# The keys of the last long attention block, made in closed tiles of 128 keys: 15 and 32 of them inside two earlier attention cores, 17 in pauses of other blocks

## The reference, cut to what matters

```python
h = layer_norm(x, g_norm)
q = h @ Wq                                 # 16 heads of 64
k, v = split(context @ Wkv)                # 2048 keys and values per batch, plus one null key and value
q, k = l2norm(q) * q_scale, l2norm(k) * k_scale
sim = einsum('bhid,bhjd->bhij', q, k) * 8.0
out = einsum('bhij,bhjd->bhid', softmax(sim), v) @ Wout
x = x + layer_norm(out, g_out)
```

## Time and profile before

| what | value |
|---|---|
| median of 3 runs | 1338.66 us (1333.35 to 1340.05) |
| the profiled execution, its own time | 1339.16 us |
| its span, first to last instruction | 1337.4 us |
| mean granted TensorE clock | 0.893 of full speed |
| PE busy | 1158.4 us, 87% of the span |
| DVE, ACT, POOL busy | 548.9, 467.1 and 434.3 us |

### The profile page before, as it was taken

The page is one execution under the profiler, slowest core; times in us unless marked ns, Lnnn a source line. Parts: engine busy times, 40 slices in busy tenths (PEclk is TensorE's granted clock), DMA queues, the critical chain, the costliest instruction groups (busy, mean ns, idle before and its releaser), DMA issues.

```text
span 1337.4 us, 15482 instructions
## 1 busy us (share of the span) xinstructions
PE 1158.4 (87%) x6398; PEld 689.3 (52%) x6398; DVE 548.9 (41%) x949; ACT 467.1 (35%) x638; POOL 434.3 (32%) x217
## 2 busy tenths in 40 slices
PE   7999967799686998987885697799999999999558
PEld 4645533265265654543472585555565555555334
DVE  2212357413344632336213512444554454454445
ACT  3344531233132554441241101544434444344111
POOL 0355500000000155520000000288687678677000
PEclk9899968899587899986896687899999999999769
DMA  8333300002000143330007003031311312210100
GB/s 350 140 144 140 142 0 1 0 1 94 33 0 1 40 158 134 126 142 0 0 1 330 0 1 126 1 126 64 126 64 64 126 64 81 109 63 1 69 0 9
DMA packets 23830, 102.74 MB, mean 77 GB/s; under 512 B 2768, under 2 KB 2768, under 8 KB 19920
## 3 DMA queue, kind: packets, MB, share of 16 engines
q1 hardware_dynamic: 23760, 101.76, 19.8%
HBM read 67.93 MB, written 33.82 MB: 76 GB/s over the span
## 4 chain that ended last, share of the span: by engine, by line
PE 77%; DVE 9%; issue 8%; ACT 4%; POOL 2%; DMA 0%; POOLq 0%; DVEq 0%; ACTq 0%
PE PSUM L1958 18%; PE PSUM L1897 10%; PE PSUM L1445 9%; PE PSUM L1534 3%; PE PSUM L1471 3%; PE PSUM L1454 2%; PE PSUM L1625 2%; PE PSUM L1636 2%; PE PSUM L1489 2%; PE PSUM L2000 1%; DVE ARENA L930 1%; PE PSUM L1822 1%; PE PSUM L1590 1%; PE PSUM L1832 1%; PE PSUM L1495 1%
## 5 line engine op out<-in xcount | busy, mean ns | idle before, releaser
L447 POOL TENSOR_TENSOR CK<-CK,ARENA 128x2048 f32<-128x2048 f32 x63 | 285.1, 4526 | 126.3 <-ACT ARENA L691 122.2
L1958 PE MATMUL PSUM<-ARENA,CT 128*128 128x512 f32 x512 | 239.7, 609 | 0.0
L1290 DVE TENSOR_TENSOR ARENA<-PSUM,RK 128x512 f32<-128x512 f32 x256 | 159.1, 684 | 186.6 <-PE PSUM L1897 186.5
L691 ACT ACTIVATE ARENA<-ARENA,WB 128x1024 f32<-128x1024 f32 x128 | 147.0, 1148 | 203.3 <-DVE ARENA L1290 200.6
L385 POOL TENSOR_TENSOR RSTD<-VE,MHALF 128x4 f32<-128x4 f32 x17 | 17.1, 1008 | 478.9 <-DVE VE L766 412.4
L1897 PEld LDWEIGHTS PSUM<-ARENA 64*128 64x128 f32 x2048 | 120.9, 190 | 50.7 <-issue 47.0
L1958 PEld LDWEIGHTS PSUM<-ARENA,CT 128*128 128x128 f32 x512 | 91.8, 190 | 99.3 <-issue 91.2
L1897 PE MATMUL PSUM<-ARENA 64*128 64x128 f32 x2048 | 133.2, 281 | 2.5 <-ACT WB L686 2.2
L1445 PE MATMUL PSUM<-CT,WK 128*128 128x512 f32 x256 | 126.8, 622 | 2.4 <-ACT W L471 1.8
L1445 PEld LDWEIGHTS PSUM<-CT,WK 128*128 128x128 f32 x256 | 43.3, 192 | 64.0 <-issue 29.5
L1429 PE MATMUL PSUM<-WA,HN 128*128 128x128 f32 x52 | 12.9, 396 | 63.4 <-DVE HN L769 49.5
(11 more groups left out here) (396 smaller groups left out, 1805.5 us busy)
## 6 DMA issues: line engine op xcount, KB each, us to landing
ARENA<-kept_keys SPq DMA_DIRECT2D x16, 2048.0 KB, 7.8
kept_keys<-KEYS SPq DMA_DIRECT2D x64, 256.0 KB, 2.0
kept_keys<-W SPq DMA_DIRECT2D x64, 256.0 KB, 2.0
CT<-in_ctxT SPq DMA_DIRECT2D x4, 1024.0 KB, 9.9
CK<-in_l0f_experts SPq DMA_DIRECT2D x1, 4096.0 KB, 22.9
CK<-in_ctxk SPq DMA_DIRECT2D x1, 4096.0 KB, 12.4
ARENA<-in_l2f_experts SPq DMA_DIRECT2D x2, 2048.0 KB, 8.4
CT<-in_ctxk SPq DMA_DIRECT2D x1, 4096.0 KB, 26.5
```

Source lines behind the costliest of these rows:

```text
L447: nc.gpsimd.tensor_tensor(LS[b % 2], LS[b % 2], PR[:, t % 2, :], ALU.add)\
L691: act(p, p, ACT.Exp, bias=SHIFT).then_inc(sem("l3x_probs"), AC.sends("l3x_probs"))
L1290: ve.tensor_tensor(PR[:, k, q * 512:(q + 1) * 512].rearrange("p (j n) -> p j n", j=4), bank(q).rearrange("p (j n) -> p j n", j=4), each(rk ...
L1958: last = mm(bank(4 + q), CTK[:, t, :], PR[:, t % 2, q * 512:(q + 1) * 512], start=k == 0, stop=k == KEY_TILES - 1)
```

## The change

The unit of work becomes a tile: 128 context rows through all eight chunks, in two halves of four matmuls of 128x128 (`key_rows`), each half filling one PSUM bank. The 64 tiles are each closed by themselves: squares of both halves, their sums in eight 32-column matmuls of 128 columns (`sum_squares`, one tile late), one transpose (`turn_norms`), and one ScalarE copy for each of the last two. `places` says where the tiles are made: 15 in the core of l0x (one for each group), 32 in the core of l1a (two for each group), 17 in pauses: three in l0a, l1x (three), ahead of l1a (two), l1f (two), l2x (one), l2a (two) and l2f (four). In l0a, ahead of l1a, in l2a and l2f they stand between the block's output and `turn_pe`, and there ScalarE squares all but the last tile itself.

There are two buffers of a whole tile for the kept keys, in place of four of a unit, and one buffer of squares for each half, in place of six in turn. Stores to HBM become 64 of 512 KB, and a load back reads four runs of 4 KB for each partition instead of one of 16 KB. The load of the last two experts of l2f into `W8` (1 MB of expert weights) and that of the contexts into `CT` move behind the last keys, as those buffers are still in use. The root and the reciprocal of the norms (`RK`) move into l2f, the latter in quarters between copies. At the end of l3x the last sums take 32 rows for each strip in one bank (L2046, L2053 of the new file), are inverted in two pieces of 256 columns, and are spread afterwards by eight small matmuls of one row (`spread_last`).

```diff
-            def key_rows(units):
-                for n in units:
-                    if n >= 2:
-                        nc.tensor.wait_ge(sem("keys_kept"), n - 1)
-                    mm(bank(5 + 2 * (n % 2)), WK[:, (n % 8) * P:(n % 8 + 1) * P], CT[:, (n // 8) * 512:(n // 8 + 1) * 512],
-                       start=True, stop=True).then_inc(sem("key_rows"), PE.sends("key_rows"))
...
+            def key_rows(s, h, bank_k):
+                if 2 * s - 1 + h > 0:
+                    nc.tensor.wait_ge(sem("keys_kept"), 2 * s - 1 + h)
+                for j in range(4):
+                    c = 4 * h + j
+                    last = mm(PSUM[:, bank_k, j * P:(j + 1) * P], WK[:, c * P:(c + 1) * P], CT[:, s * P:(s + 1) * P],
+                              start=True, stop=True)
+                last.then_inc(sem("key_rows"), PE.sends("key_rows"))
+
+            def sum_squares(s, bank_k):
+                nc.tensor.wait_ge(sem("key_squares"), 2 * s + 2)
+                if s:
+                    nc.tensor.wait_ge(sem("key_norm_rows"), s)
+                for r in range(2):
+                    for j in range(4):
+                        last = mm(PSUM[32 * j:32 * j + 32, bank_k, 0:P], w("l3x_pick")[:, 32 * r:32 * r + 32],
+                                  key_squares_of(s, r)[:, j * P:(j + 1) * P], start=r == 0, stop=r == 1, skip_group_check=True)
+                last.then_inc(sem("key_squares_added"), PE.sends("key_squares_added"))
+
+            def make_tile(s, banks, first=False):
+                a, b, n = banks
+                key_rows(s, 0, a)
+                if not first:
+                    sum_squares(s - 1, n)
+                key_rows(s, 1, b)
+                if not first:
+                    turn_norms(s - 1, n)
+
+            def make_before_turn(place, banks, first=False):
+                tiles = places[place]
+                for s in tiles[:-1]:
+                    make_tile(s, banks, first and s == tiles[0])
+                key_rows(tiles[-1], 0, banks[0])
+                key_rows(tiles[-1], 1, banks[1])
+                sum_squares(tiles[-1] - 1, banks[2])
...
             tail_pe(w("l0x_WoT"))
+            make_before_turn("l0a", (4, 5, 6), True)
...
             turn_pe()
+            turn_norms(places["l0a"][-2], 6)
...
+        L0X_TILES = 15
+        places, at = {}, 0
+        for place, n in (("l0x", L0X_TILES), ("l0a", 3), ("l1x", 3), ("l1a_norm", 2), ("l1a", 32),
+                         ("l1f", 2), ("l2x", 1), ("l2a", 2), ("l2f", 4)):
+            places[place] = range(at, at + n)
+            at += n
...
+            def keep_tile(s, banks, first, square=()):
+
+                a, b, n = banks
+                keep_key_rows(s, 0, a)
+                if 0 in square:
+                    square_keys(s, 0)
+                if not first:
+                    keep_key_sums(s - 1, n)
+                keep_key_rows(s, 1, b)
+                if 1 in square:
+                    square_keys(s, 1)
+                if not first:
+                    keep_key_norms(s - 1, n)
...
+            def key_squares(tiles, halves=(0, 1)):
+                for s in tiles:
+                    for h in halves:
+                        nc.gpsimd.wait_ge(sem("keys_kept"), 2 * s + 1 + h)
+                        if s:
+                            nc.gpsimd.wait_ge(sem("key_squares_added"), s)
+                        kept = KEEP_T[s % 2][:, h * 512:(h + 1) * 512]
+                        nc.gpsimd.tensor_tensor(key_squares_of(s, h), kept, kept, ALU.mult).then_inc(sem("key_squares"), 1)
...
                 for k in range(2):
-                    half = slice(k * 512, (k + 1) * 512)
-                    ve.reciprocal(L9INV[:, half], bank(k)).then_inc(sem("dve_step"), DV.sends("dve_step"))
...
+                    half = slice(k * 256, (k + 1) * 256)
+                    ve.reciprocal(L9INV[:, half], PSUM[:, 0, half]).then_inc(sem("l3x_inverted"), DV.sends("l3x_inverted"))
```

More of the change, by code:

```diff
@@ L308, in build, with key_squares_of, key_steps @@
         PICK2 = ARENA[0:16, 2048 + PAIRS * 3 * P:2048 + PAIRS * 3 * P + 16 * DH]
-        def key_plan(n0):
-            plan, n, added = [], n0, n0 // 4
-            for g in range(16):
[L315 to L322, removed]
+        def key_squares_of(s, h):
+            return KSQ_FIRST if h == 0 else HT[:, :] if s < L0X_TILES else WA[:, 272:784]
+        L0X_TILES = 15
[4 more added lines that the diff above has]
+            at += n
+        assert at == TILES
+        def key_steps(place):
+            left = list(places[place])
+            steps = []
+            for g in range(16):
+                if len(left) > 16 - g:
+                    steps.append((left[0], left[1]))
+                    left = left[2:]
+                else:
+                    steps.append((left[0], None) if left else (None, None))
+                    left = left[1:]
+            return steps
         SUMS_AT, VALUES_AT, OUT_AT = 0, 2, 7
@@ L346, in _, with keep_keys @@
             load(CK[:, :, :].rearrange("p a b -> p (a b)"), d["l0f_experts"], "dma_experts")
[L348 to L354, removed]
+            def keep_keys(first, last):
+                for t in range(places[first][0], places[last][-1] + 1):
+                    nc.sync.wait_ge(sem("keys_kept"), 2 * t + 2)
+                    sync.dma_start(d["keys"][t], KEEP_T[t % 2]).then_inc(sem("dma_keys%d" % (t % 2)), 16)
+            keep_keys("l0x", "l0a")
             nc.sync.wait_ge(sem("x_ready"), SP.due("x_ready", n=3))
             load(CK[:, :, :], d["ctxk"], "dma_ck")
-            keep_keys(64)
+            keep_keys("l1x", "l1a")
             nc.sync.wait_ge(sem("x_ready"), SP.due("x_ready", n=2))
-            load(W8[:, :], d["l2f_experts"][:, 14 * NW:16 * NW], "dma_moe8_early")
             load(ARENA[:, 14336:14336 + 4 * NW], d["l2f_experts"][:, 0:4 * NW], "dma_moe8_early")
+            keep_keys("l1f", "l2x")
             nc.sync.wait_ge(sem("x_ready"), SP.due("x_ready", n=2))
@@ L417, in _ @@
             norm_pool()
+            key_squares(places["l1x"], (0,))
             norm_pool()
[L421 removed]
+            key_squares(places["l1a_norm"][-1:])
+            key_squares(places["l1a"])
+            norm_pool()
+            key_squares(places["l1f"], (0,))
+            norm_pool()
+            key_squares(places["l2x"])
+            norm_pool()
+            key_squares(places["l2a"][-1:])
             norm_pool()
             norm_pool()
[L430 to L434 removed]
+            key_squares(places["l2f"][-1:])
             nc.gpsimd.wait_ge(sem("l3x_null_square"), PO.due("l3x_null_square"))
@@ L489, in core_act, with keep_before_turn @@
+            def keep_before_turn(place, banks, first=False):
+                tiles = places[place]
+                for s in tiles[:-1]:
+                    keep_tile(s, banks, first and s == tiles[0], square=(0, 1))
+                keep_key_rows(tiles[-1], 0, banks[0])
+                keep_key_rows(tiles[-1], 1, banks[1])
+                keep_key_sums(tiles[-1] - 1, banks[2])
             def core_act(groups, scale, plan=None):
                 for g in range(groups):
-                    first, second, halves, turned = plan[g] if plan else ([], [], [], [])
+                    one, two = plan[g] if plan else (None, None)
+                    last = plan and g == 15 and one is None
@@ L509, in probs @@
                         accum_out=LSUM[:, b:b + 1]).then_inc(sem("long_probs"), AC.sends("long_probs"))
+                for s in places["l1x" if masked else "l2x"]:
+                    keep_tile(s, (4, 5, 6), False, square=(1,) if masked else ())
                 probs(0)
@@ L616, in _ @@
                     .then_inc(sem("l1f_hidden_kept"), AC.sends("l1f_hidden_kept"))
+            for s in places["l1f"]:
+                keep_tile(s, (3, 4, 0), False, square=(1,))
             context_keys_act(KT, w("l2x_bk"), c0=CHUNKS // 2)
@@ L1499, in long_pe @@
                 scores(0)
+                mine = places["l1x" if masked else "l2x"]
+                for s in mine:
+                    make_tile(s, (4, 5, 6))
                 for b in range(B):
```

250 lines of the change are left out of this document (157 added, 93 removed).

## The result

The changed kernel takes 1291.28 us (median of 4, 1287.32 to 1294.27) against 1337.5 of before beside it (4 runs); the ratio is 0.9656, 95% interval 0.9618 to 0.9693. The prediction was 1295. The profiled execution of after is its fastest (1287.32, span 1285.5), that of before was above its median, so the two traces lie 51.9 us apart where the medians lie 46.2 apart.

The account below looks back on a forecast made before the run. The prediction took TensorE, with 77% of the chain's busy time, to bound the kernel. From a median of 1338.66 us, -42 + 9 - 7 - 4.4 = -44.4 gave 1295 us, range 1277 to 1323.

Parts of the forecast that it names:

- Core l0x: In l0x's core, fifteen tiles (41.0 us) replace 78.1 us of key work and 5 us of idle TensorE return: -42 us.
- Core l1a: In l1a's core, 32 tiles take 87.4 us for 78.1, stalls shrink, waits for squares come: +9 us, 0 to +21.
- Pauses: Seventeen tiles in the seven pauses: overruns cost +10 us, the clock kept up behind them gives -17, together -7.
- End of l3x: At l3x's end: sums in four strips -1.7 us, halved reciprocals -3.3, spreading adds some .6: -4.4, -5 to -3.
- At nothing: Doubled stores, loads back in 4 KB runs, later `W8` and `CT` loads, and `RK`'s root and reciprocal were put at no cost.
- Low clock in the pauses: All seventeen pause tiles run at 1.2 GHz: +49 us, 1351; at half strength 1323. Chance .03 in full, .06 at half.
- Small matmuls dearer per column: Half a tile costs over 1.42 us, so the kernel ends slower; 1373 us at twice L1636's price. Chance .02.
- A cold core: Cores l0x and l1a granted 1.2 GHz: a group takes 5 us longer in l0x, 8 in l1a. Chance .03.
- Another engine in l0x: Each group of l0x's core has a floor of 6.2 us, so the change saves 20 us less: 1315. Chance .06.
- Costly tiles: In the cores, a tile of 3.1 us, with .99 for keys and sums, adds 19 us: 1314. Chance .10.

Follow-up runs that it names:

- e5: The changed kernel run again as it is, beside three that go on from it: 1288.43 us, 0.9601 of the kernel before.
- e10: The changed kernel with the squares of l1f's two tiles made by ScalarE alone, none by GpSimd there: one run, 1290.1 us.
- e1: The kernel before with matmuls that nobody reads in its seven pauses and no key work moved: 1323.23 us, ratio 0.9843.
- e2: The changed kernel with all 64 tiles in the two cores, 32 in l0x and 32 in l1a, none in pauses: 1355.24 us, 1.0101 of before.
- e4: The changed kernel with ScalarE, not GpSimd, squaring the second half of each group's first tile in l1a's core: 1289.16 us, 0.9607 of before.
- e6: The changed kernel with one of l1a's 32 tiles made ahead of the turn of l1x's tokens: 1288.62 us, 0.9603 of before.

## Why the prediction was right, term by term

*Core l0x: -42 forecast, -43.9 measured.* The step that TensorE bounds it, and that nothing else sets a group of 4.95 us, held (4.85). A tile was 2.46 us with .15 behind it in place of 2.73: the lower bound of the working, with the exit from strips that it had left out.

*Core l1a: +9, measured +6.0.* The stall for the single buffer of squares was there at .39 a group, where .3 was put. The tile there was dearer than in l0x, by the .2 that follows strips and short scores, yet TensorE's busy time rose by 6.4, not by 9.3. In e5's profile, at a clock of .96, the core is 10.6 us longer than before, so the term lies between two profiles of one kernel.

*Pauses: -7.* The rest of the 51.9 between the profiles is -51.9 + 43.9 - 6.0 + 1.6 - 1.3 = -13.7. Overruns were forecast for l0a, l1a and l2f at 2.9, 3.5 and 3.0 and were 1.9, 1.6 and 2.8. The one of l1x, put at .2, was 3.6: there a sum waits 2.4 us for GpSimd's squares. l1f, l2x and l2a are over by 1.6, .7 and .8, in l1f partly for a reason that the working lacked, VectorE beside GpSimd (e10). That is 13 where 10 were put down, and leaves some 27 for the clock in place of 17, while e1 gives 18 without keys. By e5's profile the rest is -12.6 instead of -13.7, so that about twice the term is what both show. Not all of it is a matter of the pauses. The prediction took L1534's 9.89 us at 588.60 for a start behind a pause, 2.8 us lost; no pause work stands ahead of it. From the turn behind l1a's core to its end it is 14.6 us before and 14.6 in e1, but 11.1 in the changed kernel and 11.1 in e2, which has no tile in a pause: there the shorter time goes with the tiles that now reach to the last group of l1a's core, where the kernel before made no keys. In e5 it is 13.7. The row that the term needed is L1534 at 641.10, 2.3 us lost. With stretches that differ by 4 us between two profiles of the changed kernel (l1a from turn to turn 170.1 and 174.6), the share of each pause has no firm size.

*End of l3x: -4.4, measured -1.6, and -3.0 in e5's profile.* With the stretch behind it, that is -.2 and -3.7. This step failed in size: the working took the value matmuls (4.8 us) for covered by the reciprocals, and L1943 as staying at 2.02. With the reciprocals halved their cover went, and the projection moved as a whole behind the spread (3.62). The clock did the rest: it fell in these matmuls in the first profile, and only behind the first half of the spread in e5's.

*At nothing* held for loads and stores: DMA has 0% of the chain, and from the turn of l3x's tokens to its last sums it was 415 us in both.

*Rivals.* Low clock in the pauses: no, .83 to .92. Small matmuls dearer per column: no, .89 / 8 = .111 each for 128 columns, against .445 for 512. A cold core: no, .97 and 1.00 (.98 and .96 in e5). Another engine in l0x: none. Costly tiles: in l1a by a fifth for the keys of three halves in four, not in l0x.

The sum came to 1295 against 1291 partly by terms that cancel: the pauses gave more, the end less.

## What to carry over

Work taken out of a core that one engine bounds is worth its time there, and putting it in an idle place of that engine is worth it twice if the place also lets its clock fall: the core of l0x is 52 us shorter in the changed kernel than in e2, and matmuls that nobody reads gave 18 us in e1. Price such a move by the place and not by the form of the work, which cost some 8 us more in that core (e2). When a step is made shorter, price anew what it used to cover, as the end of l3x shows. And profile one kernel twice before a difference of a few us in one stretch is given a cause: the core of l1a differed by 4.6 us between two profiles of the changed kernel.

## What was not expected

TensorE's clock fell while TensorE was busy. The end of l3x in the changed kernel, windows of TensorE (length, busy, clock):

```profile
1190.50:1195.30 4.80, 4.80 (x46) 0.83 0.00 0
1195.30:1197.20 1.90, 1.90 (x16) 0.50 0.00 0
```

and the value matmuls of the same kernel in its second profile (e5):

```profile
1196.03:1200.09 4.06, 4.06 (x44) 1.00 0.00 0
```

In the first profile the clock falls within the value matmuls, and the spread of single rows runs at .50 throughout; in the second the same matmuls, behind the same sums in strips of 32 columns, keep 1.00, and the first half of the spread takes .64 us, where the whole took 1.91 in the first. So the narrow matmuls alone don't bring the clock down. The stretch of l2f shown with e4 is another with TensorE busy throughout, at .93 in one profile and 1.00 in the other. What sets the clock there is open.

VectorE slowed with GpSimd at work: L1184 from 2.51 to 3.35 us, back to 2.50 with GpSimd's squares taken away (e10), and in l2a the four normalisations from 1.13 to 1.85 (2.70 in e5), while in e1, which adds no GpSimd work, they take 1.12. The four L1184 of the changed kernel one by one (min/median/max in ns):

```profile
L1184 DVE TENSOR_TENSOR ARENA<-ARENA,SM x4: 685/689/1529, 588.1 to 589.9; 128x512 f32<-128x512 f32 x4
```

One of the four bears all of the .84 us. The Trainium skill ("SBUF — State Buffer", section "SBUF: two separate sides") says that the two engines share a pair of ports as an exclusive lock: where a VectorE instruction with two inputs from SBUF meets a GpSimd one that reads SBUF, the one that starts second waits until the other's instruction is over. These numbers agree with that: one instruction held, the others at their usual time.

A saving in one stretch was often not one of the whole (e4, e6), with granted clocks that differed in other stretches of equal work. No run here separates chance from cause in that.
